# A delta-rule mixer on one Trainium2 core: who transposes the growing inverse, and how wide its products are

## The reference, cut to what matters

```python
def step(S, xs):
    qt, kt, vt, gt, bt = xs
    S = S * jnp.exp(gt)[..., None, None]
    kv = jnp.einsum('bhk,bhkv->bhv', kt, S)
    delta = (vt - kv) * bt[..., None]
    S = S + jnp.einsum('bhk,bhv->bhkv', kt, delta)
    o = jnp.einsum('bhk,bhkv->bhv', qt * scale, S)
    return (S, o)
_, o = jax.lax.scan(step, S0, xs)
```

## Time and profile before

| what | value |
|---|---|
| time before, median of 3 runs | 3911.65 us (3900.70 to 3918.11) |
| span of the profiled execution, first to last instruction | 3912.5 us |
| TensorE matmul busy | 3615.0 us (92%) |
| TensorE weight load busy | 2817.6 us (72%) |
| VectorE busy | 2131.4 us (54%) |
| ScalarE busy | 1672.4 us (43%) |
| GpSimd busy | 827.5 us (21%) |
| mean granted TensorE clock | 0.973 of full |

### The profile page before, as it was taken

How to read it: one execution, slowest core, us unless ns; L and a number is a source line. 1 busy time by engine, 2 the same in 40 slices (tenths; PEclk the granted TensorE clock), 3 DMA queues, 4 the chain that set the end, 5 groups by cost and what they waited for, 6 DMA issues and landing times. The chain is left out here.

```text
span 3912.5 us, 56006 instructions
## 1 busy us (share of the span) xinstructions
PE 3615.0 (92%) x19318; PEld 2817.6 (72%) x19318; DVE 2131.4 (54%) x4279; ACT 1672.4 (43%) x3964; POOL 827.5 (21%) x569
## 2 busy tenths in 40 slices
PE   5996999996899999999999999999999996899998
PEld 2444787884677878778778787787787875787787
DVE  6673555554555555555555555555555553455454
ACT  3343223221455455554554555545555453323221
POOL 1123002000423223223232232232222211201200
PEclk8998999998999999999999999999999998899999
DMA  4003102103000000000000000000000001211110
GB/s 157 11 32 119 43 32 97 65 22 105 11 1 7 17 2 7 17 2 7 18 1 7 18 1 6 18 6 2 18 7 6 12 12 55 76 64 65 65 54 33
DMA packets 61152, 126.88 MB, mean 32 GB/s; under 512 B 3008, under 2 KB 8384, under 8 KB 59840
## 3 DMA queue, kind: packets, MB, share of 16 engines
q1 hardware_dynamic: 60864, 123.26, 9.0%
HBM read 98.09 MB, written 25.17 MB: 32 GB/s over the span
## 5 line engine op out<-in xcount | busy, mean ns | idle before, releaser
L1607 DVE COPY_PREDICATED b_Tt<-b_new_part,banks 128x256 f32<-128x256 uint8 x320 | 157.6, 493 | 557.8 <-PE banks L1858 557.8
L895 PE MATMUL banks<-f_x_hi,f_w_hi 128*128 128x512 f32 x1024 | 408.4, 399 | 43.1 <-ACT f_silu L764 23.7
L895 PE MATMUL banks<-f_x_lo,f_w_hi 128*128 128x512 f32 x1024 | 406.0, 397 | 0.0
L895 PE MATMUL banks<-f_x_hi,f_w_lo 128*128 128x512 f32 x1024 | 405.8, 396 | 0.0
L1526 DVE SCALAR_TENSOR_TENSOR b_conv<-b_raw,b_taps,b_conv 128x512 f32<-128x512 f32 x384 | 376.2, 999 | 2.9 <-ACT b_conv L1279 2.6
L1339 ACT COPY b_em<-banks 128x256 f32<-128x256 f32 x320 | 120.5, 376 | 545.0 <-PE banks L1844 545.0
L1858 PEld LDWEIGHTS banks<-b_Tt,b_em 128*128 128x128 f32 x2560 | 331.5, 192 | 23.9 <-issue 9.6
L1844 PE MATMUL banks<-b_T,b_At 128*128 128x128 f32 x2560 | 347.5, 279 | 0.5 <-ACT b_T L1330 0.5
L1858 PE MATMUL banks<-b_Tt,b_em 128*128 128x128 f32 x2560 | 341.4, 276 | 0.9 <-ACT b_em L1339 0.6
L830 DVE TENSOR_TENSOR f_h<-banks,f_silu 128x512 f32<-128x512 f32 x128 | 87.1, 689 | 435.6 <-PE banks L895 358.8
L1844 PEld LDWEIGHTS banks<-b_T,b_At 128*128 128x128 f32 x2560 | 313.4, 193 | 14.7 <-ACT b_T L1330 7.0
(11 more groups left out here) (264 smaller groups left out, 7229.2 us busy)
## 6 DMA issues: line engine op xcount, KB each, us to landing
f_x_tok<-rows SPq DMA_DIRECT2D x16, 1024.0 KB, 7.5
f_stage<-in_ffn_gate SPq DMA_DIRECT2D x8, 1024.0 KB, 6.8
f_stage<-in_ffn_up SPq DMA_DIRECT2D x8, 1024.0 KB, 8.5
f_stage<-in_ffn_down SPq DMA_DIRECT2D x8, 1024.0 KB, 4.9
f_x_res<-rows SPq DMA_DIRECT2D x8, 1024.0 KB, 5.6
f_part<-f_x_res SPq DMA_DIRECT2D x8, 1024.0 KB, 4.3
f_x_res<-f_part SPq DMA_DIRECT2D x8, 1024.0 KB, 5.6
b_w_load<-in_b_qkvz SPq DMA_DIRECT2D x8, 1024.0 KB, 6.1
```

Source lines behind the costliest of these rows:

```text
L895: mm = pe.matmul(bank, w[:, b, kind, cols], x[:, k, :], start=(k == 0 and i == 0), stop=(k == KD - 1 and i == 2))
L1607: dve.copy_predicated(half(f.Tt, i + 1, 1), new_part[:, i, :].rearrange("p (a n) -> p a n", n=LEVELS[i + 1]), half(f.right, i + 1, 1)).the ...
```

## The change

VectorE takes over the transposition. `turn_back` and TensorE's share of it go, and so do the six ScalarE copies of `turned`. In their place VectorE runs a blockwise transpose from `Tt` to `T` behind each of its own updates of `Tt`: each 32x32 block is transposed where it lies. Up to level 4, `T` is needed on its diagonal blocks of at most 32 tokens; before level 5 one more transpose moves the 32x32 block next to the diagonal. `level_x` and `level_y` of levels 0 to 4 work on the two 64x64 diagonal blocks of each unit (`corners`) and not on the whole matrix: 8 matmuls of 64x64 in place of 4 of 128x128. Level 5 keeps its products.

```diff
         HP = P // 2
+        corners = (slice(0, HP), slice(HP, P))
+        QP = P // 4
...
-            def turned(f, m, i):
-                act.wait_ge(f.s["Tps"], LV * m + i + 1)
...
-                if i == 0:
-                    act.copy(f.T[:, :, :], f.left[:, :, :]).then_inc(f.s["T0"], 1)
-                elif i < LV - 1:
-                    act.copy(half(f.T, i + 1, 0), half(f.left, i + 1, 0)).then_inc(f.s["T0"], 1)
...
+                turned(f, m, 0)
+
+            def turned(f, m, i):
+                dve.wait_ge(f.s["T"], TN * m + 1 + i)
+                if i < LV - 1:
+                    dve.transpose(flat(f.T), flat(f.Tt)).then_inc(f.s["T0"], 1)
+                else:
+                    dve.transpose(f.T[QP:HP, :, 0:QP], f.Tt[0:QP, :, QP:HP]).then_inc(f.s["T0"], 1)
 
             def level(f, m, i):
...
                 dve.copy_predicated(half(f.Tt, i + 1, 1), new_part[:, i, :].rearrange("p (a n) -> p a n", n=LEVELS[i + 1]),
                                     half(f.right, i + 1, 1)).then_inc(f.s["T"], 1)
+                turned(f, m, i + 1)
...
-            def turn_back(f, m, i):
...
+            def level_x(f, m, i):
+                pe.wait_ge(f.s["T0"], LV * m + i + 1)
+                pe.sem_inc(s["pe_gate"], 1)
                 for u in range(U):
                     if i < LV - 1:
-                        mm = pe.matmul(f.wide[:, u, :], f.At[:, u, :], f.T[:, u, :], start=True, stop=True)
+                        for d in corners:
+                            mm = pe.matmul(f.wide[d, u, d], f.At[d, u, d], f.T[d, u, d], start=True, stop=True)
...
                 for u in range(U):
                     if i < LV - 1:
-                        mm = pe.matmul(f.right[:, u, :], f.X[:, u, :], f.Tt[:, u, :], start=True, stop=True)
+                        for d in corners:
+                            mm = pe.matmul(f.right[d, u, d], f.X[d, u, d], f.Tt[d, u, d], start=True, stop=True)
...
                 for i in range(2, LV):
                     f, b = flights[(i - 2) // 2], i % 2
-                    turn_back(A, m, i)
                     z(f, b, LOW)
                     level_y(B, m, i - 2)
                     level_x(A, m, i)
-                    turn_back(B, m, i - 1)
                     z(f, b, HIGH)
                     level_y(A, m, i)
                     level_x(B, m, i - 1)
```

More of the change, by code:

```diff
@@ L1060, in __init__ @@
                     "ktok", "vtok", "ktoks", "vtoks", "kqs", "qss", "at", "atm", "pt", "T0", "diag",
-                    "T", "Tps", "px", "X", "py", "rhs", "pd", "d", "pod", "dend", "ps", "o", "xf", "sqs",
+                    "T", "px", "X", "py", "rhs", "pd", "d", "pod", "dend", "ps", "o", "xf", "sqs",
                     "ssq", "sse2", "rn", "rnq", "xn", "txn", "xnT", "po", "acc")}
@@ L1320, in values @@
                                    ).then_inc(f.s["vtoks"], 1)
-            def turned(f, m, i):
-                act.wait_ge(f.s["Tps"], LV * m + i + 1)
-                if i == 0:
-                    act.wait_ge(f.s["xf"], m)
-                act.wait_ge(f.s["px"], LV * m + i)
-                if i == 0:
-                    act.copy(f.T[:, :, :], f.left[:, :, :]).then_inc(f.s["T0"], 1)
-                elif i < LV - 1:
-                    act.copy(half(f.T, i + 1, 0), half(f.left, i + 1, 0)).then_inc(f.s["T0"], 1)
-                else:
-                    act.copy(f.T[0:HP, :, 0:HP], f.left[0:HP, :, 0:HP]).then_inc(f.s["T0"], 1)
             def level(f, m, i):
@@ L1381, in pair @@
                 tokens(B, m)
-                turned(A, m, 0)
                 if not last:
@@ L1388, in pair @@
                 values(B, m)
-                turned(A, m, 1)
                 level(A, m, 1)
@@ L1392, in pair @@
                     first_tap(1, m + 1)
-                turned(B, m, 0)
                 level(B, m, 0)
                 for i in range(2, LV):
-                    turned(A, m, i)
                     if i == 2 and not last:
@@ L1401, in pair @@
                     level(A, m, i)
-                    turned(B, m, i - 1)
                     if 2 <= i <= 3 and not last:
@@ L1408, in pair @@
                 from_state(A, m)
-                turned(B, m, LV - 1)
                 if not last:
@@ L1823, in products @@
                 mm.then_inc(f.s["at"], 1)
-            def turn_back(f, m, i):
-                if i == 0:
-                    pe.wait_ge(f.s["pt"], m + 1)
-                pe.wait_ge(f.s["T"], TN * m + 1 + i)
-                if i == LV - 1:
-                    pe.sem_inc(s["pe_gate"], 1)
+            def level_x(f, m, i):
+                pe.wait_ge(f.s["T0"], LV * m + i + 1)
+                pe.sem_inc(s["pe_gate"], 1)
                 for u in range(U):
                     if i < LV - 1:
-                        mm = pe.transpose(f.left[:, u, :], f.Tt[:, u, :], ident[:, :])
-                    else:
-                        mm = pe.transpose(f.left[0:HP, u, 0:HP], f.Tt[0:HP, u, 0:HP], ident[0:HP, 0:HP])
-                mm.then_inc(f.s["Tps"], 1)
-            def level_x(f, m, i):
-                pe.wait_ge(f.s["T0"], LV * m + i + 1)
-                if i == LV - 1:
-                    pe.sem_inc(s["pe_gate"], 1)
-                for u in range(U):
-                    if i < LV - 1:
-                        mm = pe.matmul(f.wide[:, u, :], f.At[:, u, :], f.T[:, u, :], start=True, stop=True)
+                        for d in corners:
+                            mm = pe.matmul(f.wide[d, u, d], f.At[d, u, d], f.T[d, u, d], start=True, stop=True)
                     else:
@@ L1935, in pair @@
                 v(0, HIGH)
-                turn_back(A, m, 0)
                 products(B, m)
@@ L1941, in pair @@
                 v(1, [1])
-                turn_back(A, m, 1)
                 v(1, [2])
@@ L1945, in pair @@
                 v(1, [3])
-                turn_back(B, m, 0)
                 level_y(A, m, 1)
@@ L1963, in pair @@
                 qk(0, 0)
-                turn_back(B, m, LV - 1)
                 qk(0, 1)
```

## The result

The changed kernel takes 3820.24 us (median of 4 runs, 3812.27 to 3824.16) against 3910.73 of the kernel before on the same chip: ratio 0.977 [0.975, 0.979], 90 us less. The forecast was 3685, so 227 less: right in sign, and two and a half times too much. The profiled execution of the changed kernel has a span of 3822.2.

A forecast was written before the change was run, and what follows sets the result against it. TensorE was taken as the bound, busy 68.33 of a pair's 70.40 us. Gains of 1.5 + 4.8 + 0.8 = 7.1 us a pair, times 32, is 227: 3912.5 - 227 = 3685 us, range 3645 to 3832.

The forecast's parts named there:

- Part 1: Transposes leave TensorE: saves 0.44 us and the wait, ten times a pair, and a smaller one twice.
- Part 2: Level products on 64x64 blocks: 0.60 us each, between 0.46 and 0.93, plus 0.2 a half round for changes of form.
- one after the other: Rival: the two blocks' matmuls don't overlap, a product takes 0.93 us, the kernel 3810 us; chance 0.20.
- drain at each change: Rival: each switch between array quarters costs 0.1 us, a product takes 1.63, the kernel 4137 us; chance 0.11.
- Part 3: Transposes on VectorE: 0.70 us for each 128x512 transpose.
- Where the levels begin: Up to A's level_x 2: TensorE idles some 1.5 us before B's level_x 0, yet 1.5 us a pair is gained.
- the clock falls: Rival: idle where levels begin and in the first round lowers TensorE's clock, 3.5 us a pair lost, 3797 us; chance 0.12.
- First round: Taps stretched beside GpSimd's subtractions make this round 5.5 us; all rounds 14.6 instead of 19.4, gain 4.8 us a pair.
- Behind the levels: From level_x 5 to from_state: 2.9 us instead of 3.79, gain 0.9 a pair, of which 0.1 is given back.
- The sum: Gains of 1.5 + 4.8 + 0.8 = 7.1 us a pair, times 32 is 227 us.
- transpose at 1.28 us: Rival: a VectorE transpose takes 1.28 us, gain only 2.8 us a pair, the kernel 3822 us; chance 0.06.
- two signs of being wrong: Granted clock under 1.00 in the middle of a pair, or VectorE without idle time in the rounds.

The follow-up runs named there:

- by_block: Changed kernel with all first 64x64 diagonal blocks of a product ahead of all second ones, instead of alternating: 3866.06 us, ratio 0.989 to the kernel before.
- late_xcur: Changed kernel with GpSimd's copy of `x_cur` held back until A's end state is formed: 3738.99 us, ratio 0.956 to the kernel before.
- taps_behind: Changed kernel with the two taps ahead of A's level 5 copy moved behind it, GpSimd's copy left in place: 3737.18 us, ratio 0.956.
- delayed: Changed kernel with late `x_cur` copy and taps away from GpSimd's subtractions, plus three useless VectorE transposes ahead of A's level 5 copy: 3748.24 us.

## Why the prediction was wrong, point by point

**Part 1 and Part 2** held. The prices from the timeline (z 0.86, 0.1 for each change of form, 16 matmuls side by side) gave 2.26 a half round, and 2.14 was measured. I took 0.60 for a product between 0.46 and 0.93; from level_y to level_x it is 0.52, of which eight steps of 58 ns are 0.46, and by_block shows that the reason is the alternation of quarters. So the products overlap in full, and *one after the other* and *drain at each change* fall; the changes of form cost some 0.35 a half round and not 0.20. The rule that I quoted from the Trainium skill, TensorEngine Tiling (Array Packing), Restrictions and Gotchas, against two row tiles in one PSUM bank at the same time is not borne out here: the two blocks of a unit go to one bank, to different partitions of it, and their matmuls start 6 to 7 ns apart. The rule quoted from the Trainium skill, TensorE: Matmul & The Clock Gate, Part 3, of some 4 ns between the starts of two tiles, was nearer.

**Part 3** held: 0.70 was forecast and 0.71 measured, 320 times. The group of line L1588 in the changed kernel (busy us, mean ns, idle before; answers to the earlier trace rows):

```profile
L1588 DVE STREAM_TRANSPOSE b_T<-b_Tt 128x512 f32<-128x512 f32 x320 | 227.7, 712 | 11.0
```

**Where the levels begin** held: 9.50 where the forecast had 9.6. TensorE waits 1.09 before B's level_x 0 instead of 1.5, and behind it the clock stays at 1.00 in the first 31 pairs, so *the clock falls* was wrong about this place.

**First round** was half right. The forecast let A's level 2 stand behind the stretched taps and counted 14.6 for the rounds. In the 8 pairs without a lower clock or a second wait it is 14.66, but by two errors that cancel: the first round takes 6.28 and not 5.5, since TensorE waits 1.84 and not about 1, and the next two take 8.38 and not 9.1. In 16 other pairs the clock falls behind the wait and the rounds take 16.2; in 6 the subtractions for the weights make them 15.5. The mean gain is 3.8 and not 4.8: some 32 of the 137 us that are missing.

**Behind the levels** is the step that failed. It took the tap's 0.74 for the taps at A's level 5 and did not ask what GpSimd does there. The copy of `x_cur` waits for z's end and is as free to move as TensorE's list is; with z earlier and the taps later they met. A gain of 0.8 was forecast. Measured is a loss of 1.25 up to from_state and of 1.10 behind it, 0.91 of that by the clock and 0.19 by the change of form: 3.15 us a pair against the forecast, 101 us, most of what is missing. The same mechanism stood in the earlier trace rows, and the first round used it: there it was read off as a number for one place and not as a property of GpSimd's work wherever it runs. late_xcur and taps_behind bring back 81 and 83 us, and pair 31, where GpSimd copies nothing, has neither the stretch nor the lower clock.

**The sum** of 227 lies near the 252 that the change is worth with the collisions out of the way, but in part by chance: the forecast had one collision in its 14.6 for the rounds, which are 12.64 without it, and it left out 0.2 for the change of form and 0.5 in the rest of the pair. The *clock* rival had a mechanism that is there, and came near the time (3797), but only one of its two places, the first round, was right; the other is behind the levels. By the rows the clock costs 16 x 1.55 = 25 us in the rounds and 31 x 0.91 = 28 behind the levels, 53 us and not 115; much of the other loss is the waits themselves. The *transpose at 1.28 us* came nearest, with 3822, by luck: the transpose takes 0.71. Of the two signs of being wrong that the prediction named, the clock under 1.00 in the middle of a pair came true (0.92); VectorE was without idle time in the first round alone, busy for 6.22 of the 6.29 us of the second window.

Settled is that the collisions hold the levels, that idle time lowers the clock, and that the quarters run side by side. Open is why the same wait of 2.4 us lowers the clock in 25 pairs of delayed and not in the other 7, and what makes the rest of a pair 0.4 us longer in the changed kernel (35.25 against 34.83), 13 us that no run here looks into.

## What to carry to other kernels

When a change makes one engine's list shorter, list every instruction of the other engines that is released by that engine, and see beside what it will now run; here a GpSimd copy that nobody waits for at that moment cost some 82 us. A stretched instruction in the trace of before is a property of the pair of instructions, so look for each place where the two can meet once the order moves. Two good halves can be worth less together than one of them, until the fillers around them are placed again.

## What the runs showed of the hardware that was not expected

GpSimd's copy does not slow the two taps evenly. In the changed kernel the instructions of L1510 and of L1155 in the stretch behind the levels: count, ns min/median/max, first and last start, forms.

```profile
L1510 DVE SCALAR_TENSOR_TENSOR b_conv<-b_raw,b_taps,b_conv x1: 709/709/709, 1276.4 to 1276.4; 128x512 f32<-128x512 f32 x1
L1510 DVE SCALAR_TENSOR_TENSOR b_conv<-b_raw,b_taps,b_conv x1: 2378/2378/2378, 1277.1 to 1277.1; 128x512 f32<-128x512 f32 x1
L1155 POOL COPY b_x_cur<-b_xT x1: 2242/2242/2242, 1276.6 to 1276.6; 128x2048 f32<-128x2048 f32 x1
```

The first tap began before the copy and took its 709 ns; the copy took 2.24 instead of 1.89; the second tap took 2378 ns and ended 0.6 us after the copy did. These times read as if the two took turns: in taps_behind the copy began ahead of the taps and took its 1.89. The Trainium skill says so in SBUF — State Buffer, Who interferes with whom: a VectorE instruction with two SBUF inputs contends with a GpSimd instruction that reads SBUF, and their shared ports are an exclusive lock. The trace agrees. By the same section of the Trainium skill a VectorE instruction with at most one SBUF input does not contend with GpSimd, outside certain modes. The trace agrees: the 128x512 transposes of the changed kernel take 0.711 to 0.715, the 112 with GpSimd at work beside them like the 208 without. The masked copies, with the mask as their input from SBUF, aren't stretched either: those of level 0 take 0.72 to 0.75 and the others 0.39 to 0.45, beside GpSimd or not.

The order of independent matmuls in the list is worth 0.3 us a product: 16 of 64x64 with the two blocks in alternation against block after block.
